# An attention and expert layer on one core: a rearranged prologue, with the layer norm applied by ScalarE

## The chip, the cores and the metric
The kernel runs on one core of a Trainium2 chip. The core has five engines, each with its own queue that runs in order: TensorE (PE, matmuls and transposes, with its weight loads PEld), VectorE (DVE), ScalarE (ACT), GpSimd (POOL) and SyncE (SP, which issues most DMAs). They wait for each other by semaphores. The metric is the device time of one execution in microseconds; the median of three runs of the kernel before is 842.51 us (841.69 to 844.74).

## The reference, cut to what matters
```python
mod = silu(c) @ wmod                       # c: (4, 256); six vectors of 256 per batch
sa, ca, ga, sb, cb, gb = ...               # ga, gb: sign kept, magnitude at least 0.25
h = layernorm(x) * (1 + ca) + sa           # x: (4, 512, 256)
q, k, v = (einsum('ihd,bpd->biph', W, h) for W in (W_Q, W_K, W_V))   # 16 heads of 128
attn = softmax(causal(k . q) / sqrt(128))  # 512 x 512 for each batch and head
x = x + ga * (W_O . (attn @ v))
h = layernorm(x) * (1 + cb) + sb
d = h @ down_w + down_b                    # to 128 columns
probs = softmax(h @ router_w + router_b - cost);  top 2 of 8 experts, gate = softmax(top)
# each of the 8 experts, hidden 128 to 512:
acc_e = gelu(gelu(d or 0) @ w1 + b1) @ w2 + b2
out = sum(gate * acc_e) + 0.1 * shared(d)
x = x + gb * (out @ up_w + up_b + gelu(h) @ core_w + core_b)
```
An expert that a token didn't choose still gives gelu(b1) @ w2 + b2 there; the kernel computes gelu(b1) once ("b1"), builds masked copies of it ("d0") and multiplies them with w2 ("dta", "dt").

## The kernel before, in words
All matmuls are fp32 products made of three fp32r matmuls (`mm3`, lines 679 to 682): each operand is held as a high part, written by ScalarE as a cast to fp32r, and a residual, written by VectorE or GpSimd as the difference. So nearly every product is followed by a ScalarE copy and a VectorE subtraction (L639 and L1049 for q, k, v and z; L619, L620 and L1035 for h; L609 with L532 or L987 for weights).

The work is a list of events (`plan`) made by `attention_plan` and `ffn_plan`. Every engine walks the same list and issues its own part of each event, so the list sets each engine's order. PSUM banks for events of `MISC` rotate over three: a product waits until the bank's use three before has been read.

The attention has 64 units (4 groups of 4 heads x 4 batches x 4 heads). A unit has: "q", "k" (PE), "v" (one half for each unit of a pair), "S" (scores in four row blocks; VectorE adds the mask and takes the row minimum at L1060, ScalarE exponentiates at L591), "ri" (reciprocal of the sums), "norm" (ScalarE scales the probabilities, L626), "ty" (VectorE transposes 32x32 blocks, L1076 to L1079), "tr" (four DMAs that complete the transpose, L462), "pt" (high part by ScalarE, L650; residual by GpSimd, L547), "z" (probabilities times v, PE) and "wo" (output product; VectorE multiplies by the gate ga, L1089, GpSimd adds to x, L540). Step i of the main loop has S(i+2), q(i+3), k(i+3), wo, v, pt(i+1), z(i) and tr(i+2); `pre` events stand ahead of z(i), `fill` groups after S, q, wo, z or v, and `post` events at the end.

A batch's layer norm is "st" 0 to 3 (VectorE's statistics L1004, L1009, L1013; GpSimd's power -1/2 at L490), "nm" 0 and 1 (VectorE writes (x - mean) * rstd to `tmp`, four instructions of 256 columns at L1025) and "h" 0 and 1 (PE transposes, L730; ScalarE applies scale and shift). "n" 0 to 3 are the batches' first norms, 4 to 7 their second. Norm 4 stands in step 55, norm 5 in step 59, norm 6 in step 62, just ahead of "dn 0" (the first batch's down projection, whose two gelus ScalarE does at L656 and L658 after loading another activation table). Norm 7 is in the expert stage.

The prologue's list is: b1, mod0, the statistics of batch 0, silu, wh0, wh1, nm, mod, h, wh2, then units 0 and 1 and wh3. "mod" makes the first layer's scale and shift, "ms" the second's and "mg" the gates ga and gb. For "mg" VectorE copies the product to `rows` (L974 to L977), and GpSimd then makes max(|g|, 0.25) with its sign in five dependent instructions (L497 to L505), writes it to DRAM with two DMAs, waits for them and issues the broadcast load (L508 to L511). "mg" and "ms" read the second part of wmod, which lies in x's place of batches 2 and 3; SP loads these batches after "ms". "mg" and batch 1's "h" come at the end of step 0, "ms" at the end of step 1. "wh n" and "ld n" take piece n of the weights through `stage`.

Before the first real product PE runs `warm(56)`, after "mod" `warm(4)` and after h(0) `warm(18)`: small bf16 matmuls on zeros.

Of the kernel before, what the change touches and what calls it, by code (L numbers as in the profile page):

```python
# [8 lines left out]
ALU = mybir.AluOpType  # L9
ACT = mybir.ActivationFunctionType  # L10
AX = mybir.AxisListType

B, S, D, H, DH = 4, 512, 256, 16, 128
# [4 lines left out]
EXPERT = [e for e, h in enumerate(HID) for _ in range(h // 128)]  # L18
LAG = 3
EULER = 2.718281828459045  # L20
WARM = 56, 4, 18
INV = 1.0 / float(DH) ** 0.5
BIG = 3.0e38

# [20 lines left out]
def attention_plan():  # L45

    pre, post = {}, {}
    fill = {}

    def put(where, i, *events):  # L50
        where.setdefault(i, []).extend(events)

    put(post, 0, ("mg",))
    put(post, 1, ("ms",))
    for b in (1, 2, 3):
        i = (0, 2, 5)[b - 1]
        if b == 1:
            fill[i] = [[("st", b, 0), ("st", b, 1)], [("st", b, 2)], [("st", b, 3)], [("nm", b, 0), ("nm", b, 1)]]
            put(post, i, ("h", b, 0), ("h", b, 1))
            continue  # L60
        fill[i] = [[("st", b, 0)], [("st", b, 1)], [("st", b, 2)], [("st", b, 3)]]
        fill[i + 1] = [[("nm", b, 0)], [("nm", b, 1)]]
        put(post, i + 1, ("h", b, 0))
        put(post, i + 2, ("h", b, 1))
    for n in range(4, 16):
        put(pre, 16 * (n // 4 - 1) + 5 + 2 * (n % 4), ("wh", n))
    for n in range(16, 20):
        put(pre, 34 + n, ("wh", n))
    fill[20] = [[("d0", 0)], [("d0", 1)], [], [], [("d0", 2)]]
    for b in range(2):  # L70
        fill[54 + 4 * b] = [[("st", B + b, k)] for k in range(4)]
        fill[55 + 4 * b] = [[("nm", B + b, 0)], [("nm", B + b, 1)]]
        put(post, 55 + 4 * b, ("h2", b, 0))
        put(post, 56 + 4 * b, ("h2", b, 1))
        put(post, 57 + 4 * b, ("r", b))
    fill[58] = [[("rs", 0, 1), ("rs", 0, 2)]] + fill[58]
    put(post, 58, *[("rp", 0, c) for c in range(4)])
    fill[59] += [[], [("rs", 0, 3)], [("rs", 0, 4)]]
    fill[60] = [[("rs", 0, k)] for k in range(5, 10)]
    fill[61] = [[("rs", 0, k)] for k in range(10, 15)]  # L80
    put(post, 61, ("wt", 0))
    fill[62] = [[("st", 6, 0), ("st", 6, 1)], [("st", 6, 2)], [("st", 6, 3)], [("nm", 6, 0), ("nm", 6, 1)]]
    put(post, 61, ("wh", 20), ("ld", 22))
    plan = [("b1",), ("mod0",)] + [("st", 0, k) for k in range(4)] + [("silu",), ("wh", 0), ("ld", 2), ("wh", 1), ("ld", 3),
            ("nm", 0, 0), ("nm", 0, 1), ("mod",),
            ("h", 0, 0), ("h", 0, 1), ("wh", 2), ("ld", 4), ("q", 0), ("k", 0), ("v", 0, 0), ("S", 0), ("ri", 0), ("norm", 0), ("ty", 0), ("q", 1), ("k", 1), ("v", 0, 1),
            ("S", 1), ("q", 2), ("ri", 1), ("k", 2), ("norm", 1), ("ty", 1), ("tr", 0), ("tr", 1), ("pt", 0), ("wh", 3)]
    loads = {0: [5]}
    for i, events in pre.items():
        for ev in events:  # L90
            if ev[0] == "wh":
                loads.setdefault(i + 1, []).append(ev[1] + 2)
    for i in range(NU):
        steps = list(fill.get(i, []))

        def add(*events):
            for ev in events:
                plan.append(ev)
                if steps and ev[0] in ("S", "q", "wo", "z", "v"):
                    plan.extend(steps.pop(0))  # L100

        if i + 2 < NU:
            add(("S", i + 2))
        if i + 3 < NU:
            add(("q", i + 3))
        if i + 2 < NU:
            add(("ri", i + 2))
        if i + 3 < NU:
            add(("k", i + 3))
        if i + 2 < NU:  # L110
            add(("norm", i + 2))
        if i >= 2:
            add(("wo", i // 2 - 1, i % 2))
        if i + 2 < NU:
            add(("ty", i + 2), ("v", i // 2 + 1, i % 2))
        if i + 1 < NU:
            add(("pt", i + 1))
        add(*pre.get(i, []))
        add(("z", i))
        if i + 2 < NU:  # L120
            add(("tr", i + 2))
        plan += [("ld", n) for n in loads.get(i, [])]
        plan += [ev for group in steps for ev in group]
        plan += post.get(i, [])
        if i + 2 == NU:
            plan.append(("dn", 0))
    return plan


def ffn_plan():  # L130
# [4 lines left out]
    def put(t, j, *events):  # L135
        at.setdefault((t, j), []).extend(events)
# [2 lines left out]
    put(0, 0, ("rs", 1, 1))  # L139
    put(0, 1, ("rs", 1, 2), ("wo", last, 0))  # L140
    put(0, 2, ("wo", last, 1), ("wl", 0), ("wl", 1))
    put(0, 3, ("wh", 22))
    put(0, 4, ("h2", 2, 0))
    put(0, 5, ("h2", 2, 1), ("wl", 2), ("wl", 3))
    for k, j in enumerate((6, 7, 8, 9)):
# [35 lines left out]
    plan, later = [], []  # L181
# [30 lines left out]
def build(nc, x, ct, wmod, wat, wfa, wfb, cst, bcol, b2, ub, cb, out, scr, scw):  # L212
    plan = attention_plan() + ffn_plan()
    use, rd = {}, {}
# [18 lines left out]
    with ExitStack() as ctx:  # L233
# [3 lines left out]
        def sem(name):  # L237
            return ctx.enter_context(nc.semaphore(name))
# [3 lines left out]
        X = sb("X", 4096)  # L242
        tmp = sb("tmp", 1024)
        fb = sb("fb", 1024)
        stage = sb("stage", 2048)
        cc = sb("cc", C_END)
# [6 lines left out]
        mv = sb("mv", 8 + 24)  # L253
        rs = sb("rs", 16)
        sm = sb("sm", 4)
        nb = sb("nb", 4)
        ri = sb("ri", 4)
# [32 lines left out]
        mask = cc[:, C_MASK:C_MASK + 512]  # L290

        s_x = [sem(f"s_x{b}") for b in range(B)]
        s_ct, s_wm, s_wm2, s_c, s_b, s_bc, s_g, s_gb = (sem(n) for n in ("s_ct", "s_wm", "s_wm2", "s_c", "s_b", "s_bc", "s_g", "s_gb"))
        s_st = [sem("s_st0"), sem("s_st1")]
        s_wh, s_wl, s_wd = sem("s_wh"), sem("s_wl"), sem("s_wd")
        s_sil, s_mod, s_mc, s_gr, s_gd = (sem(n) for n in ("s_sil", "s_mod", "s_mc", "s_gr", "s_gd"))
        mf, mh, me = sem("mf"), sem("mh"), sem("me")
# [4 lines left out]
        s_ve, s_r0, s_xn = sem("s_ve"), sem("s_r0"), sem("s_xn")  # L302
# [25 lines left out]
        def wt(slot, at, n):  # L328
            return W[slot][:, at:at + n], W[slot][:, 4096 + at:4096 + at + n]
# [73 lines left out]
        def piece_after(n):  # L403
# [3 lines left out]
                return ("wo", 8 * (n // 4) - 9, 1)  # L407
            return ("v", NU // 2 - 1, 1)

        block = ctx.enter_context(nc.Block())  # L410


        @block.sync
        def _(sp):
# [4 lines left out]
            def load_x(b):  # L419
                sp.dma_start(X[:, b * 1024:b * 1024 + 1024], x[:, b * 1024:b * 1024 + 1024]).then_inc(s_x[b], 16)  # L420

            load_x(0)
            load(0)
            sp.dma_start(cc[:, 0:128], cst[:, 0:128]).then_inc(s_id, 16)
            load(1)
            sp.dma_start(cc[:, 128:], cst[:, 128:]).then_inc(s_c, 16)
            for ev in plan:
                if ev[0] == "ms":
                    sp.wait_ge(mf, use[ev] + 1)
# [2 lines left out]
                elif ev[0] == "wh":  # L432
                    n = ev[1]
                    if n == 2:
                        sp.dma_start(X[:, 2048:4096], wmod[:, 1024:3072]).then_inc(s_wm2, 16)
                        load_x(1)
                elif ev[0] == "ld":
                    n = ev[1]
                    sp.wait_ge(s_wl, n - 2) if n > 2 else sp.wait_ge(s_wd, 1)
# [138 lines left out]
        def _(act):  # L578
# [16 lines left out]
            for ev in plan:  # L595
# [7 lines left out]
                elif kind == "wh":  # L603
# [3 lines left out]
                    if piece_after(n):  # L607
                        act.wait_ge(mf, use[piece_after(n)] + 1)
                    act.copy(wt(slot, a, w)[0], stage[:, (n % 2) * 1024:(n % 2) * 1024 + w]).then_inc(s_wh, 1)  # L609
                elif kind in ("h", "h2"):  # L610
                    _, b, k = ev
                    o = 0 if kind == "h" else 16
# [268 lines left out]
        def _(v):  # L881
# [75 lines left out]
                v.tensor_tensor(sil[:, 16:24], sil[:, 16:24], sil[:, 0:8], ALU.mult).then_inc(s_sil, 1)  # L957


            tmp_read = [use[("h", b, 1)] + 1 for b in range(B)] + [use[("h2", b, 1)] + 1 for b in range(B)]  # L960
            xv = 0
            for ev in plan:
                kind = ev[0]
# [27 lines left out]
                elif kind == "st":  # L991
# [3 lines left out]
                    if k == 0:  # L995
                        if n < B:
                            v.wait_ge(s_x[b], 16)
                        else:
                            v.wait_ge(s_y, 2 * (25 + 2 * b) + 2)
                        if n:  # L1000
                            v.wait_ge(s_xn, 2 * n)
                    if k < 2:
                        for c in (2 * k, 2 * k + 1):
                            ins = v.bn_stats(mv[:, 8 + 6 * c:14 + 6 * c], X[:, b * 1024 + 256 * c:b * 1024 + 256 * c + 256])  # L1004
                        ins.then_inc(s_st_, 1)
                    elif k == 2:
                        v.wait_ge(s_st_, 3 * n + 2)
                        for c in range(4):
                            ins = v.bn_aggr(mv[:, 2 * c:2 * c + 2], mv[:, 8 + 6 * c:14 + 6 * c])  # L1009
                        ins.then_inc(s_st_, 1)  # L1010
                    else:
                        v.wait_ge(s_st_, 3 * n + 3)
                        v.tensor_scalar(rs[:, 0:4], mv[:, 1:8:2], 1e-5, None, ALU.add).then_inc(s_ve, 1)  # L1013
                elif kind == "nm":

                    _, n, k = ev
                    b = n % B
                    dst = stage[:, 0:1024] if n == 7 else tmp[:]
                    if n == 7:
                        v.wait_ge(s_wd, 3)  # L1020
                    elif n:
                        v.wait_ge(mf, tmp_read[n - 1])
                    v.wait_ge(s_r0, n + 1)
                    for c in (2 * k, 2 * k + 1):
                        ins = v.tensor_scalar(dst[:, 256 * c:256 * c + 256],  # L1025
# [255 lines left out]
```

## Time and profile before
| | us |
|---|---|
| median of 3 runs | 842.51 (841.69 to 844.74) |
| profiled execution, its own time | 843.71 |
| its span, first to last instruction | 841.9 |
| mean granted TensorE clock | 0.978 |

Durations below come from the profiled execution. A timeline row is: start, duration, engine, line, operation, output<-input, shapes, number of instructions merged, and in brackets how long the engine had been idle and what released it. Clock 1.00 is 2.4 GHz, 0.50 is 1.2 GHz.

### The profile page before, as it was taken

What the parts mean: (1) busy time and instruction counts of PE and PEld (TensorE: products, weight loads), DVE (VectorE), ACT (ScalarE), POOL (GpSimd) and SP (SyncE); (2) the same over time, 40 slices, a digit from 0 to 9 for tenths busy, and PEclk for the clock granted to TensorE, in tenths of its full rate; (3) what the DMA queues carried; (4) which work ended last, traced back from release to release, by engine and by line L of the source; (5) the groups of instructions that cost most, each with busy time, mean ns of one, the idle gap of its engine ahead of it and who ended that gap; (6) DMA issues with size and microseconds to landing.
All of it is one profiled execution on the core that took longest, in us unless ns stands there. A gap on an engine that the chain in (4) does not pass through costs nothing.

```text
span 841.9 us, 14484 instructions
## 1 busy us (share of the span) xinstructions
PE 800.9 (95%) x4822; PEld 713.0 (85%) x4822; DVE 680.8 (81%) x1639; ACT 628.3 (75%) x1404; POOL 450.2 (53%) x311
## 2 busy tenths in 40 slices
PE   7778999999999999999999999999999599999997
PEld 6657978999999999999999999998998587788786
DVE  4686998888888888888888788889898787877776
ACT  4566778878887788788887887787877488686874
POOL 3064455664444655544466544575465555566753
PEclk7979999999999999999999999999999799999999
DMA  7233223334222433332234332344222220212131
GB/s 243 72 89 107 63 63 88 88 97 111 63 64 65 112 94 88 91 89 66 64 89 108 100 88 63 78 107 129 65 63 64 69 84 18 76 51 80 47 114 38
DMA packets 47449, 70.54 MB, mean 84 GB/s; under 512 B 5520, under 2 KB 38448, under 8 KB 47248
## 3 DMA queue, kind: packets, MB, share of 16 engines
q1 hardware_dynamic: 46720, 68.28, 30.8%
q0 software_dynamic: 368, 0.81, 0.3%
q8 instruction: 39, 0.64, 0.3%
q10 hardware_dynamic: 288, 0.53, 0.2%
q14 instruction: 34, 0.28, 0.1%
HBM read 25.49 MB, written 2.17 MB: 33 GB/s over the span
## 4 chain that ended last, share of the span: by engine, by line
PE 75%; ACT 9%; DVE 8%; issue 3%; POOL 2%; DMA 2%; SPq 0%; DVEq 0%; POOLq 0%; ACTq 0%
PE M L681 16%; PE M L680 16%; PE M L682 16%; PE S L680 7%; PE S L682 6%; PE S L681 6%; ACT PB L591 3%; PE T L680 2%; PE T L682 2%; PE T L681 2%; ACT PB L626 1%; DVE tmp L1025 1%; DVE S L1060 1%; DVE gab L1076 1%; ACT pth L650 1%
## 5 line engine op out<-in xcount | busy, mean ns | idle before, releaser
L547 POOL TENSOR_TENSOR ptl<-ptl,pth 128x640 fp32r<-128x640 f32 x128 | 198.9, 1576 | 45.0 <-ACT pth L650 45.0
L591 ACT ACTIVATE PB<-S,nb 128x128 f32<-128x128 f32 (+3 forms) x256 | 133.8, 532 | 114.0 <-DVE nb L1060 114.0
L540 POOL TENSOR_TENSOR X<-X,fb 128x512 f32<-128x512 f32 x64 | 83.2, 1301 | 252.1 <-DVE fb L1089 252.1
L626 ACT ACTIVATE PB<-PB,ri 128x256 f32<-128x256 f32 (+3 forms) x256 | 124.4, 579 | 9.4 <-DVE ri L1069 9.3
L1049 DVE TENSOR_TENSOR qk<-M,qk 128x512 fp32r<-128x512 f32 x128 | 88.1, 689 | 53.5 <-ACT qk L639 53.5
L1060 DVE CUSTOM_DVE_ANT_0 S<-S,cc 128x128 f32<-128x128 f32 (+3 forms) x256 | 117.5, 521 | 2.3 <-PE S L682 2.3
L1076 DVE STREAM_TRANSPOSE gab<-PB 128x256 f32<-128x256 f32 (+2 forms) x192 | 109.5, 623 | 1.1 <-ACT PB L626 0.6
L680 PE MATMUL M<-hh,W 128*128 128x512 f32 x264 | 103.8, 393 | 0.2 <-DVE hl L1035 0.2
L681 PE MATMUL M<-hl,W 128*128 128x512 f32 x264 | 103.3, 391 | 0.0
L682 PE MATMUL M<-hh,W 128*128 128x512 f32 x264 | 103.1, 391 | 0.0
L680 PE MATMUL S<-qk 128*128 128x128 f32 (+3 forms) x256 | 88.0, 344 | 4.6 <-DVE qk L1049 4.6
L650 ACT CAST pth<-ptl 128x640 fp32r<-128x640 f32 x128 | 87.7, 743 | 3.5 <-DMA ptl<-gab 3.5
L673 ACT ACTIVATE Gr<-S,bc 128x512 fp32r<-128x512 f32 x84 | 58.5, 696 | 34.3 <-PE S L682 34.3
L682 PE MATMUL S<-qk 128*128 128x128 f32 (+3 forms) x256 | 83.5, 326 | 0.0
L681 PE MATMUL S<-qk 128*128 128x128 f32 (+3 forms) x256 | 83.4, 326 | 0.0
L681 PE MATMUL M<-ptl,vh 128*128 128x512 f32 (+3 forms) x256 | 83.4, 326 | 0.0
L682 PE MATMUL M<-pth,vl 128*128 128x512 f32 (+3 forms) x256 | 83.0, 324 | 0.0
L1203 DVE TENSOR_TENSOR Gr<-S,Gr 128x512 fp32r<-128x512 f32 x84 | 57.4, 687 | 31.2 <-ACT S L674 29.1
L680 PE MATMUL M<-pth,vh 128*128 128x512 f32 (+3 forms) x256 | 81.0, 316 | 1.6 <-DVE qk L1049 1.1
L639 ACT CAST qk<-M 128x512 fp32r<-128x512 f32 x128 | 75.9, 594 | 6.7 <-PE M L682 6.4
L680 PE MATMUL M<-W,hh 128*128 128x256 f32 x256 | 73.6, 287 | 6.5 <-DVE qk L1049 6.1
L681 PE MATMUL M<-W,hh 128*128 128x256 f32 x256 | 72.7, 284 | 0.0
(181 smaller groups left out, 2310.5 us busy)
## 6 DMA issues: line engine op xcount, KB each, us to landing
ptl<-gab SPq DMA_DIRECT2D x256, 160.0 KB, 3.1
stage<-in_wat SPq DMA_DIRECT2D x16, 512.0 KB, 4.9
gab<-scw SPq DMA_DIRECT2D x16, 256.0 KB, 3.3
tmp<-scw SPq DMA_DIRECT2D x16, 256.0 KB, 3.5
X<-in_x SPq DMA_DIRECT2D x4, 512.0 KB, 5.3
stage<-in_wfa SPq DMA_DIRECT2D x3, 512.0 KB, 4.4
out<-X SPq DMA_DIRECT2D x3, 512.0 KB, 2.6
X<-in_wmod SPq DMA_DIRECT2D x1, 1024.0 KB, 6.5
```

The lines of the kernel that those rows point to most:

```text
L540: pool.tensor_tensor(X[:, a:a + 512], X[:, a:a + 512], fb[:, c2 * 512:c2 * 512 + 512], ALU.add).then_inc(s_y, 1)
L547: pool.tensor_tensor(ptl[u % 2][:, s], ptl[u % 2][:, s].bitcast(F32), pth[u % 2][:, s].bitcast(F32), ALU.subtract).then_inc(s_pl, 1)
L591: ins = act.activation(PB[:, P_OFF[i]:P_OFF[i] + w], PS[bk][:, a:a + w], ACT.Exp, bias=nb[:, i:i + 1], scale=-1.0, accum_out=sm[:, i:i + 1])
L626: act.activation(p, p, ACT.Copy, scale=ri[:, i:i + 1]).then_inc(s_P3, 1)
L639: act.copy(dst, src).then_inc(mh, 1)
L650: act.copy(pth[u % 2][:, s], ptl[u % 2][:, s].bitcast(F32)).then_inc(s_ph, 1)
L680: pe.matmul(o, lhs[0], rhs[0], start=start, stop=False, **kw)
L681: pe.matmul(o, lhs[0], rhs[1], start=False, stop=False, **kw)
L682: return pe.matmul(o, lhs[1], rhs[0], start=False, stop=stop, **kw)
L1049: v.tensor_tensor(lo, src, hi.bitcast(F32), ALU.subtract).then_inc(me, 1)
L1060: ins = v.tensor_tensor_reduce(PS[bk][:, a:a + w], PS[bk][:, a:a + w], mask[:, 512 - w:512], -INV, BIG, ALU.add, ALU.min, nb[:, i:i + 1])
L1076: v.transpose(Y_blocks(i, i + 1), P_blocks(i, 0, i + 1))
```

## The change
- "b1" leaves the head of the list and is done in the expert stage, at chunk 3; the three "d0" operations move from step 20 to chunks 5 to 7.
- x of batch 0 is loaded in two halves with a semaphore each; the identity is loaded ahead of the first weight piece; x of batch 1 is loaded with the first transfers.
- The layer norm is applied by ScalarE for norms 0 to 6: a new event "nb" has VectorE compute -mean * rstd for the four row blocks, and "nm" is then four ScalarE activations with scale and bias from `rs`. Norm 7 stays on VectorE.
- Batch 1's statistics and norm go into the prologue; its h half 0 stands ahead of z(0), half 1 at the end of step 0, after "ms".
- "mg" goes into the prologue, behind v(0,1) and ahead of wh3 and pt(0); "ms" goes to the end of step 0.
- In the prologue v(0,0) and v(0,1) come after "ty", tr(0) right after v(0,0), and wh1 stands behind the norm of batch 0.
- The warm-up counts are 60, 4, 12.

```diff
-WARM = 56, 4, 18
+WARM = 60, 4, 12
...
-    put(post, 0, ("mg",))
-    put(post, 1, ("ms",))
+    put(post, 0, ("ms",))
     for b in (1, 2, 3):
         i = (0, 2, 5)[b - 1]
         if b == 1:
-            fill[i] = [[("st", b, 0), ("st", b, 1)], [("st", b, 2)], [("st", b, 3)], [("nm", b, 0), ("nm", b, 1)]]
-            put(post, i, ("h", b, 0), ("h", b, 1))
+            put(pre, i, ("h", b, 0))
+            put(post, i, ("h", b, 1))
             continue
         fill[i] = [[("st", b, 0)], [("st", b, 1)], [("st", b, 2)], [("st", b, 3)]]
-        fill[i + 1] = [[("nm", b, 0)], [("nm", b, 1)]]
+        fill[i + 1] = [[("nb", b), ("nm", b, 0)], [("nm", b, 1)]]
...
-    fill[20] = [[("d0", 0)], [("d0", 1)], [], [], [("d0", 2)]]
...
-        fill[55 + 4 * b] = [[("nm", B + b, 0)], [("nm", B + b, 1)]]
+        fill[55 + 4 * b] = [[("nb", B + b), ("nm", B + b, 0)], [("nm", B + b, 1)]]
...
-    fill[62] = [[("st", 6, 0), ("st", 6, 1)], [("st", 6, 2)], [("st", 6, 3)], [("nm", 6, 0), ("nm", 6, 1)]]
+    fill[62] = [[("st", 6, 0), ("st", 6, 1)], [("st", 6, 2)], [("st", 6, 3)], [("nb", 6), ("nm", 6, 0), ("nm", 6, 1)]]
...
-    plan = [("b1",), ("mod0",)] + [("st", 0, k) for k in range(4)] + [("silu",), ("wh", 0), ("ld", 2), ("wh", 1), ("ld", 3),
-            ("nm", 0, 0), ("nm", 0, 1), ("mod",),
-            ("h", 0, 0), ("h", 0, 1), ("wh", 2), ("ld", 4), ("q", 0), ("k", 0), ("v", 0, 0), ("S", 0), ("ri", 0), ("norm", 0), ("ty", 0), ("q", 1), ("k", 1), ("v", 0, 1),
-            ("S", 1), ("q", 2), ("ri", 1), ("k", 2), ("norm", 1), ("ty", 1), ("tr", 0), ("tr", 1), ("pt", 0), ("wh", 3)]
+    plan = [("mod0",)] + [("st", 0, k) for k in range(4)] + [
+        ("silu",), ("nb", 0), ("wh", 0), ("ld", 2), ("nm", 0, 0), ("nm", 0, 1), ("wh", 1), ("ld", 3), ("mod",),
+        ("h", 0, 0), ("h", 0, 1), ("st", 1, 0), ("st", 1, 1), ("wh", 2), ("ld", 4),
+        ("q", 0), ("st", 1, 2), ("st", 1, 3), ("k", 0), ("nb", 1), ("nm", 1, 0), ("nm", 1, 1), ("S", 0),
+        ("q", 1), ("ri", 0), ("k", 1), ("norm", 0), ("ty", 0), ("v", 0, 0), ("tr", 0),
+        ("S", 1), ("q", 2), ("ri", 1), ("k", 2), ("norm", 1), ("ty", 1), ("v", 0, 1), ("mg",),
+        ("wh", 3), ("tr", 1), ("pt", 0)]
...
-    put(0, 3, ("wh", 22))
+    put(0, 3, ("wh", 22), ("b1",))
+    for k in range(3):
+        put(0, 5 + k, ("d0", k))
...
-            load_x(0)
+            for n, done in enumerate((s_x[0], s_xh)):
+                sp.dma_start(X[:, 512 * n:512 * n + 512], x[:, 512 * n:512 * n + 512]).then_inc(done, 16)
+            sp.dma_start(cc[:, 0:128], cst[:, 0:128]).then_inc(s_id, 16)
             load(0)
-            sp.dma_start(cc[:, 0:128], cst[:, 0:128]).then_inc(s_id, 16)
             load(1)
             sp.dma_start(cc[:, 128:], cst[:, 128:]).then_inc(s_c, 16)
+            load_x(1)
...
                     if n == 2:
                         sp.dma_start(X[:, 2048:4096], wmod[:, 1024:3072]).then_inc(s_wm2, 16)
-                        load_x(1)
...
+                elif kind == "nm" and ev[1] < 7:
+                    _, n, k = ev
+                    b = n % B
+                    act.wait_ge(s_nb, n + 1)
+                    if n and k == 0:
+                        act.wait_ge(mf, tmp_read[n - 1])
+                    for c in (2 * k, 2 * k + 1):
+                        s = slice(b * 1024 + 256 * c, b * 1024 + 256 * c + 256)
+                        ins = act.activation(tmp[:, 256 * c:256 * c + 256], X[:, s], ACT.Identity,
+                                             bias=rs[:, 8 + c:9 + c], scale=rs[:, 4 + c:5 + c])
+                    ins.then_inc(s_xn, 1)
...
+                    if n == 0 and k == 1:
+                        v.wait_ge(s_xh, 16)
...
+                elif kind == "nb":
+                    n = ev[1]
+                    v.wait_ge(s_r0, n + 1)
+                    v.scalar_tensor_tensor(out=rs[:, 8:12], in0=mv[:, 0:8:2], scalar=-1.0, in1=rs[:, 4:8],
+                                           op0=ALU.mult, op1=ALU.mult).then_inc(s_nb, 1)
```

## Rows read from the trace of the kernel before

**Rows 1.** the page's busy time, share of the span, instructions of each engine
```profile
PE 800.9 (95%) x4822; PEld 713.0 (85%) x4822; DVE 680.8 (81%) x1639; ACT 628.3 (75%) x1404; POOL 450.2 (53%) x311
```

**Rows 2.** busy us (x instructions) of PE, PEld, DVE, ACT, POOL; clock, DMA, GB/s
```profile
34.00:36.00 2.00, 2.00 (x7) 1.81 (x8) 0.58 (x3) 0.00 (x0) 0.00 (x0) 0.50 0.90 223
...
100.00:200.00 100.00, 97.22 (x613) 88.15 (x613) 86.30 (x207) 79.94 (x192) 54.66 (x35) 1.00 0.35 87
...
680.00:690.00 10.00, 9.27 (x46) 7.27 (x45) 8.70 (x16) 9.99 (x18) 3.82 (x4) 1.00 0.43 131
```

**Rows 3.** timeline (start, us, engine, line, output<-input, idle before), prologue
```profile
11.10 1.04 ACT L609 CAST W<-stage 128x1024 fp32r<-128x1024 f32 x1 [0.72 <-DMA stage<-in_wat]
11.56 3.49 DVE L1025 TENSOR_SCALAR tmp<-X,mv,rs 128x256 f32<-128x256 f32 x4
...
19.12 0.69 DVE L1035 TENSOR_TENSOR hl<-M,hh 128x512 fp32r<-128x512 f32 x1 [0.65 <-ACT M L620]
```

**Rows 4.** the DMA issued within 1.1 to 1.3 us; last: us to landing
```profile
stage<-in_wat SPq DMA_DIRECT2D x1, 512.0 KB, 7.2
```

**Rows 5.** timeline of PE, 26 to 100 us
```profile
33.30 0.48 PE L680 MATMUL S<-qk 128*128 128x128 f32 x1 [2.96 <-DVE qk L1049]
...
47.70 0.50 PE L680 MATMUL M<-pth,vh 128*128 128x512 f32 x1
...
57.50 1.94 PE L730 MATMUL M<-cc,tmp 128*128 128x128 f32 x8 [5.85 <-DVE tmp L1025]
...
69.35 1.90 PE L719 MATMUL M<-sil,X 128*128 128x4 f32 x16
...
80.32 0.38 PE L680 MATMUL M<-W,hh 128*128 128x256 f32 x1 [2.92 <-DVE qk L1049]
```

**Rows 6.** timeline of POOL (GpSimd), 10 to 100 us
```profile
43.10 3.11 POOL L547 TENSOR_TENSOR ptl<-ptl,pth 128x640 fp32r<-128x640 f32 x2 [20.66 <-ACT pth L650]
46.17 2.40 POOL L532 TENSOR_TENSOR W<-stage,W 128x1024 fp32r<-128x1024 f32 x1
...
58.53 1.95 POOL L497 TENSOR_SCALAR gab<-rows 4x512 f32<-4x512 f32 x1 [1.97 <-DVE rows L977]
...
69.17 0.57 POOL L511 DMA_DIRECT2D gab<-scr  x1 [1.37 <-DMA scr<-rows]
```

**Rows 7.** timeline of DVE (VectorE), 27 to 650 us
```profile
43.95 0.26 DVE L1060 CUSTOM_DVE_ANT_0 S<-S,cc 128x128 f32<-128x128 f32 x1
...
57.68 0.67 DVE L977 COPY rows<-M 4x512 f32<-4x512 f32 x1
...
62.10 0.29 DVE L1060 CUSTOM_DVE_ANT_0 S<-S,cc 128x128 f32<-128x128 f32 x1
...
78.92 0.75 DVE L1004 BATCH_NORM_STATS2 mv<-X 128x6 f32<-128x256 f32 x2 [4.65 <-DMA X<-in_x]
...
86.67 0.29 DVE L1060 CUSTOM_DVE_ANT_0 S<-S,cc 128x128 f32<-128x128 f32 x1
...
121.98 2.19 DVE L1025 TENSOR_SCALAR tmp<-X,mv,rs 128x256 f32<-128x256 f32 x2
...
648.58 0.28 DVE L1060 CUSTOM_DVE_ANT_0 S<-S,cc 128x128 f32<-128x128 f32 x1
```

**Rows 8.** ACT (ScalarE) groups by form: busy us, mean ns, idle before
```profile
L626 ACT ACTIVATE PB<-PB,ri 128x256 f32<-128x256 f32 x64 | 34.5, 539 | 9.4 <-DVE ri L1069 9.3
...
L619 ACT ACTIVATE hh<-M,modt 128x512 fp32r<-128x512 f32 x16 | 12.7, 794 | 11.5 <-PE M L730 10.6 <-POOL X L540 0.9
```

**Rows 9.** timeline of ACT, POOL, DVE and PE at the hand-over
```profile
667.46 1.28 ACT L656 ACT_TABLE_LOAD   x1
...
670.04 1.02 POOL L490 TENSOR_TENSOR rs<-rs 128x4 f32<-128x4 f32 x1
...
671.17 1.38 DVE L1025 TENSOR_SCALAR tmp<-X,mv,rs 128x256 f32<-128x256 f32 x4 [2.52 <-POOL rs L490]
...
673.21 0.50 PE L680 MATMUL S<-ur,W 128*128 128x512 f32 x1 [0.86 <-DVE ur L1189]
```

More of the change, by code:

```diff
@@ L292, in build @@
         s_x = [sem(f"s_x{b}") for b in range(B)]
+        s_xh, s_nb = sem("s_xh"), sem("s_nb")
         s_ct, s_wm, s_wm2, s_c, s_b, s_bc, s_g, s_gb = (sem(n) for n in ("s_ct", "s_wm", "s_wm2", "s_c", "s_b", "s_bc", "s_g", "s_gb"))
@@ L408, in piece_after @@
             return ("v", NU // 2 - 1, 1)
+        tmp_read = [use[("h", b, 1)] + 1 for b in range(B)] + [use[("h2", b, 1)] + 1 for b in range(B)]
         block = ctx.enter_context(nc.Block())
@@ L957, in silu @@
                 v.tensor_tensor(sil[:, 16:24], sil[:, 16:24], sil[:, 0:8], ALU.mult).then_inc(s_sil, 1)
-            tmp_read = [use[("h", b, 1)] + 1 for b in range(B)] + [use[("h2", b, 1)] + 1 for b in range(B)]
             xv = 0
@@ L1013, in _ @@
                         v.tensor_scalar(rs[:, 0:4], mv[:, 1:8:2], 1e-5, None, ALU.add).then_inc(s_ve, 1)
-                elif kind == "nm":
+                elif kind == "nb":
[3 more added lines that the diff above has]
+                                           op0=ALU.mult, op1=ALU.mult).then_inc(s_nb, 1)
+                elif kind == "nm" and ev[1] == 7:
                     _, n, k = ev
                     b = n % B
[L1018 to L1022, printed above, removed]
+                    dst = stage[:, 0:1024]
+                    v.wait_ge(s_wd, 3)
                     v.wait_ge(s_r0, n + 1)
```

## The prediction
> **What bounds the kernel now.** I read the busy shares first. The tensor engine is busy for 95% of the span [rows 1], so what can be won is PE's idle time and the time it runs at half clock. Then the table of stretches: from 100 to 200 us PE is busy for 97.22 of 100 us, at full clock, while ScalarE (ACT) has 79.94 and VectorE (DVE) 86.30 [rows 2]. So between about 90 and 650 us the order of PE's own work sets the pace, and a change on another engine counts there only where it starves PE. Third, the chain of waits and PE's own timeline for the first 100 us, where PE stands still four times for reasons that this change touches:
> - before its first real matmul: the first batch's transposed layer norm is ready only when the last VectorE residual starts at 19.12 us, that is at 19.8 [rows 3];
> - 2.96 us before unit 1's scores, behind a k residual [rows 5];
> - 5.85 us before the transposes of batch 1, behind its layer norm [rows 5];
> - 2.92 us before a v product; its cause is VectorE's 4.65 us wait for batch 2 of x to land, with the k residual queued behind it [rows 5, 7].
> After the stop of 2.96 us PE's granted clock is 0.50, 1.2 GHz in place of 2.4 (34 to 36 us) [rows 2].
> Last, the hand-over from attention to experts, from 666 us. PE's first expert matmul starts at 673.21 us and waited for VectorE's residual of the down projection [rows 9].
>
> **The change, part by part.** The profiled execution took 843.71 us (span 841.9 us and 1.8 around it), 1.2 above the median of the three runs. I work out a difference, and add it to the median.
>
> *Start.* The gelu of b1 and its activation table leave the head of ScalarE's queue; the exp of silu now comes first. The copy of weight piece 0 can start when its piece has landed, at 1.2 + 7.2 = 8.4 us [rows 4]. Two issues and the identity now stand ahead of this load, so I take 8.7. Copy (1.04, as piece 1's) to 9.7, then ScalarE applies the layer norm. The trace has no ScalarE instruction of that form. Bounds: 539 ns for 256 columns with a scale alone, 794 ns for 512 columns with bias and scale [rows 8]; four lie between 2.0 and 3.2 us, and as neighbours overlap by some 0.1 us I take 2.0, nearest to the 256-column row. VectorE's four took 3.49 us here [rows 3]. The norm ends at 11.7 in place of 15.05. ScalarE then does the copy of piece 1 (it landed at 11.1, copy 1.04 [rows 3]) to 12.7, and the two halves of h follow as before. The last residual ends at 16.4 in place of 19.8: 3.4 us gained.
> The Trainium skill, "ScalarE: Activation LUTs", section "What ACT_TABLE_LOAD costs", gives 186 ns + 0.833 ns per element and about 93 ns per pointer operand. By that one of these would be an estimated 585 ns, four 2.1 us with its overlap of 93 ns; the 794 ns of the 512-column row agree (its formula gives 799).
>
> *Up to unit 1.* Batch 1's statistics (two pairs, 1.4 us) and its norm lie beside PE's q, k and scores. Because "v" goes behind the scores and transposes, unit 1's scores no longer stand behind a k residual that waited for the transposes: the 2.96 us go. VectorE's transposes of unit 1 ended at 43.95, where unit 2's scores start [rows 7]; now 43.95 - 3.4 - 2.9 = 37.7.
>
> *The gate.* "mg" now comes right there: v residual 0.65, two small operations and the copy of the gate rows (0.67 [rows 7]), 1.1 in all: ends at 39.4. From this copy's end (57.68 + 0.67 = 58.35) to the last of GpSimd's gate instructions (69.17 + 0.57 = 69.74 [rows 6]) go 11.4 us: five operations, two transfers out, a wait for them, one transfer back. GpSimd's queue is in order. Before, that stretch lay between the probability residuals of unit 1 and those of unit 2 and held up little. Now piece 3's residual (2.40) and unit 0's probability residuals (3.11) are queued behind it [rows 6]: 39.4 + 11.4 + 2.4 + 3.1 = 56.3. PE's first attention product z(0), which ran at 47.70 [rows 5], waits for them. So it starts 8.6 us later than before, after some 13 us of idle PE and at half clock. This is a new wait, worth more than each of those removed.
>
> *From z(0) to unit 3's scores on VectorE.* Before: 47.70 to 62.10, 14.4 us, with the 5.85 us wait for batch 1's norm in it [rows 5, 7]; that wait goes, as the norm was made in the prologue. After: z(0) has 3 x 1280 columns, at 1.2 GHz 3.3 us; the second modulation product 2.6 (1.90 at full clock [rows 5], twice that at half; I take a clock that rises in between); four transposes 0.7, a third of the eight at 57.50 (1.94); then ScalarE and VectorE on h half 1, 2.1: 8.7 us, to 65.0. Against 62.10 that is 2.9 us late; all that the start gained is spent.
>
> *Units 3 and 4.* The modulation is read out of x's place a unit earlier, so batch 2's load is issued at about 63 and lands by 69, before VectorE asks (about 76). From unit 3's to unit 5's scores it was 86.67 - 62.10 = 24.6 us. A unit without a stop: (648.58 - 86.67)/58 = 9.69 us [rows 7]. Two are 19.4: 5.2 gained. Net at unit 5: -2.3 us.
>
> *Norms of batches 2, 3 and of the second layer norm.* ScalarE 2.0 us more in four units (with h its queue holds 11.7 us in such a unit against 9.69), VectorE 1.4 less (1.38 for four at 671.17 [rows 9]) up to 4.4 less (2.19 for two beside GpSimd [rows 7]). PE buffers a unit. I take +0.3; bounds -2 and +4 (one us each way per unit, the full difference of 11.7 and 9.7 being 2).
>
> *Hand-over.* Batch 2's second norm. GpSimd's pow runs 670.04 to 671.06, then VectorE normalised 671.17 to 672.47, and ScalarE meanwhile loaded gelu's table at 667.46 and did the down projection's gelus [rows 9]. Now the norm stands in ScalarE's queue ahead of that: it waits for the small VectorE operation to 671.3, takes 2.0 to 673.3, table 1.28, two gelus 1.3, residual 0.6: PE's first expert matmul starts at 676.5 in place of 673.21, 3.3 late. PE then has idled 4.3 us, more than the 2.96 after which it was seen at half clock; at half clock its next two to three products cost 1.2 more. From 680 to 690 ScalarE is busy for 9.99 of 10 us and PE for 9.27 [rows 2], so little is caught up: 0.5. +4.0 us; bounds +1 and +6. If the shift reached no end it would be 0.
>
> *Gelu of b1 and the three "d0" operations* among the experts: 0.2 on ScalarE, under 1 on VectorE, both with slack; +0.2. The warm-up matmuls (60 and 12 for 56 and 18) move within idle time, 0; bounds -0.7 and +1 (a head of PE at half clock).
>
> Sum: -2.3 + 0.3 + 4.0 + 0.2 = +2.2, the profiled execution to 845.9, the median to 844.7. 0.5% is 4.2 us, about what a measurement of this kernel tells from no change: my forecast is no measurable change.
>
> **Rivals.**
> A. *The gate hides on GpSimd* (its operations run quicker beside an idle VectorE, or the copy comes earlier). Then z(0) starts at 43 to 50, and each us is a us of time: from -3 to -13 at unit 3. For it: GpSimd has been idle for 20.66 us when unit 0's probabilities reach it at 43.10 [rows 6]. Against: 3.4 of the 11.4 us are transfers, and the copy needs unit 1's transposes. With a third of it hidden, -8: 836.5. Chance 0.15.
> B. *The hand-over's delay is absorbed*: PE was idle 0.86 there and stops again later, ScalarE has room after 690. +1 in place of +4: 841.5. Chance 0.2.
> C, on the other side: *ScalarE becomes the bound in each unit that holds a norm.* Place: behind unit scores 5, 8, 57, 61; the norm delays the exponentials, these the k copy and the normalised probabilities. It decides as soon as PE's lead is used up: then each costs 11.7 - 9.7 = 2.0 less what VectorE's relief gives, some +1.3, 5 in all: 849.5. For it: the queue's 11.7 against 9.69. Against: ScalarE is busy for 80% only from 100 to 200 us [rows 2], and a lead of PE carries a late unit over. Chance 0.2. The Trainium skill, "ScalarE: Activation LUTs", "Rules for kernel authors", says adds and multiplications belong on VectorE; by that rule this rival holds. The trace agrees only where GpSimd rests: 1.38 us for four on VectorE at 671.17 [rows 9], 3.49 beside GpSimd's and others' work [rows 3].
> Forecast: 0.45.
>
> **Numbers.** Faster by over 0.5% (below 838.3): A's 0.13 and 0.05 of B and the forecast, 0.18. Slower by over 0.5% (above 846.7): C 0.17 and 0.07 of the forecast, 0.24. Within: 0.58. The range reaches to A and C and holds the bounds of the norm and the hand-over: 835.5 to 850.0; the forecast's own is 841 to 848.
>
> **What would show it.** VectorE's first h residuals end near 16.4; the gate copy at 39; GpSimd's gate run ends near 51; PE idle some 12 us up to z(0) near 56, at 0.50 clock after it; no stop of VectorE for x; unit 5's scores near 84.4; four ScalarE norms of 0.5 us each near 671, and the table load behind them; first expert matmul 1.3 us later in the span than before (674.5). Wrong, if z(0) starts before 52, if the first expert matmul's distance to the end of attention doesn't grow, or if PE idles in units 3 and 6.

## The result and the profile after

The changed kernel takes 858.9 us (median of 4 runs, 855.3 to 859.6), the kernel before 842.9 us: ratio 1.0176, 95% interval 1.0154 to 1.0197. It is 16 us slower by the medians. I had forecast 844.7 us, no measurable change, in a range from 835.5 to 850.0; the time is 8.9 us above its upper end.

The profiled execution took 859.18 us against 843.71, so the two traces, 15.5 us apart, show nearly the whole of it. First the page of the profile: PE's busy share, and its granted clock in 40 slices of 21.4 us.

```profile
span 857.4 us, 14481 instructions
PE 807.3 (94%) x4820; PEld 717.1 (84%) x4820; DVE 664.5 (77%) x1618; ACT 640.4 (75%) x1431; POOL 449.5 (52%) x311
PEclk8958999999999999999999999999998788999999
```

Before, the line of the clock was:

```profile
PEclk7979999999999999999999999999999799999999
```

PE is busy 6.4 us longer than before [rows 1] for the same products: part of the loss is work at half clock, in slices 3 and 4 (43 to 86 us) and 31 to 34 (643 to 729 us). PE's longest waits in the new kernel (total, times, longest):

```profile
PE M L699 <- POOL ptl L554: 13.6, 2, 13.1
PE M L878 <- DVE wg L969: 9.2, 2, 7.1
PE M L699 <- DVE qk L1072: 7.4, 9, 0.9
PE S L699 <- DVE ur L1212: 4.4, 1, 4.4
```

The first and the fourth are new at this length (before, the same two were 0.5 and 0.9 us). The waits of 2.96, 5.85 and 2.92 us of before [rows 5] are gone, as is VectorE's of 4.65 us for x [rows 7].

To see where time is lost I follow one set of events through every trace: the start of PE's first attention product z(0), of VectorE's first score operation of units 3, 5 and 63, and of ScalarE's first gelu of expert chunks 0, 9 and 15. It is read from timelines; the last column is the end of the span.

```
                     z(0)   unit 3  unit 5  unit 63  chunk 0  chunk 9  chunk 15   span
before               47.70   62.10   86.67   648.58   674.21   689.38    703.10  841.9
changed              57.09   67.27   86.94   650.95   680.76   697.33    718.55  857.4
later by              9.39    5.17    0.27     2.37     6.55     7.95     15.45   15.5
```

So the attention up to its last unit costs 2.4 us, the hand-over to the experts 5.6 more (4.2 to chunk 0, 1.4 to chunk 9), and 7.5 come in a stretch where I had expected 0.2. GpSimd's timeline in the first 100 us shows the gate ahead of the probabilities:

```profile
40.44 1.95 POOL L504 TENSOR_SCALAR gab<-rows 4x512 f32<-4x512 f32 x1 [18.56 <-DVE rows L995]
...
51.03 0.57 POOL L518 DMA_DIRECT2D gab<-scr  x1 [1.36 <-DMA scr<-rows]
51.62 2.35 POOL L539 TENSOR_TENSOR W<-stage,W 128x1024 fp32r<-128x1024 f32 x1
53.92 6.01 POOL L554 TENSOR_TENSOR ptl<-ptl,pth 128x640 fp32r<-128x640 f32 x4
```

These answer to [rows 6]. PE's timeline, against [rows 5, 9]:

```profile
57.09 0.77 PE L699 MATMUL M<-pth,vh 128*128 128x512 f32 x1 [13.08 <-POOL ptl L554]
...
679.07 0.79 PE L699 MATMUL S<-ur,W 128*128 128x512 f32 x1 [4.42 <-DVE ur L1212]
...
699.03 0.25 PE L865 MATMUL M<-g0z,W 128*128 128x16 f32 x1 [1.31 <-issue]
```

The hand-over on VectorE (-mean * rstd) and ScalarE, against [rows 9]:

```profile
673.40 0.16 DVE L1038 SCALAR_TENSOR_TENSOR rs<-mv,rs 128x4 f32<-128x4 f32 x1 [2.43 <-POOL rs L497]
673.60 2.07 ACT L626 ACTIVATE tmp<-X,rs 128x256 f32<-128x256 f32 x4 [3.84 <-DVE rs L1038]
675.69 1.28 ACT L675 ACT_TABLE_LOAD   x1
680.76 0.69 ACT L692 ACTIVATE Gr<-S,bc 128x512 fp32r<-128x512 f32 x1 [2.02 <-PE S L701]
```

And the stretches of the new loss (columns as in [rows 2]; the eighth number, ahead of the DMA share, is the clock), with the VectorE instruction that PE waited for at 699.03, the last of "d0" (the trace names no releaser there; in the kernel `dta` waits for that instruction's semaphore, and it ends at 698.93):

```profile
50.00:60.00 10.00, 2.91 (x9) 2.66 (x10) 0.00 (x0) 0.00 (x0) 8.88 (x6) 0.50 0.16 53
60.00:70.00 10.00, 10.00 (x42) 9.44 (x42) 3.43 (x12) 3.02 (x7) 0.00 (x0) 0.52 0.70 195
690.00:700.00 10.00, 8.45 (x42) 6.31 (x41) 9.23 (x17) 8.67 (x15) 3.81 (x3) 1.00 0.41 134
700.00:710.00 10.00, 10.00 (x41) 8.89 (x41) 3.09 (x10) 2.48 (x4) 7.48 (x6) 0.55 0.08 28
710.00:720.00 10.00, 9.99 (x37) 6.85 (x37) 4.74 (x11) 4.95 (x8) 1.29 (x1) 0.77 0.02 9
730.00:740.00 10.00, 7.83 (x33) 5.46 (x33) 9.64 (x20) 7.72 (x14) 6.63 (x5) 1.00 0.12 39
```

```profile
697.92 1.01 DVE L1134 TENSOR_TENSOR g0z<-g,g0z 128x160 fp32r<-128x160 f32 x1
```

From 700 to 710 PE is busy all the time, ScalarE and VectorE are idle two thirds of it and more, and the clock is 0.55: PE does its products at half clock.

### The profile page after: what moved, and what is told of

Its sections match the earlier page's. It is cut to its first block, busy times and chain, and to the rows that moved or that the text cites. A ratio compares the mean times of both kernels' runs of the same rounds, so it can differ in the third digit from the quotient of the medians.

```text
span 857.4 us, 14481 instructions
## 1 busy us (share of the span) xinstructions
PE 807.3 (94%) x4820; PEld 717.1 (84%) x4820; DVE 664.5 (77%) x1618; ACT 640.4 (75%) x1431; POOL 449.5 (52%) x311
## 4 chain that ended last, share of the span: by engine, by line
PE 72%; ACT 13%; DVE 9%; issue 3%; POOL 2%; DMA 1%; SPq 0%; DVEq 0%; ACTq 0%; POOLq 0%
PE M L699 15%; PE M L700 15%; PE M L701 15%; PE S L699 6%; PE S L701 6%; PE S L700 6%; ACT PB L598 4%; PE T L699 2%; PE T L701 2%; PE T L700 2%; ACT qk L658 2%; DVE S L1083 2%; ACT tmp L626 2%; DVE gab L1099 1%; ACT PB L645 1%
## 5 line engine op out<-in xcount | busy, mean ns | idle before, releaser
L699 PE MATMUL M<-pth,vh 128*128 128x512 f32 (+3 forms) x256 | 81.4, 318 | 17.2 <-POOL ptl L554 13.6
L699 PE MATMUL M<-W,hh 128*128 128x256 f32 x256 | 73.1, 286 | 3.9 <-DVE qk L1072 3.9
L699 PE MATMUL M<-W,zt 128*128 128x256 f32 x256 | 72.9, 285 | 0.0
```

The costliest lines, as they stand in the source:

```text
L699: pe.matmul(o, lhs[0], rhs[0], start=start, stop=False, **kw)
```

## The experiments

Times are medians; each was measured beside the kernel before, whose medians were 843.0 to 844.1. The differences are to the changed kernel's 858.9. The event times in the tables are those of one profiled execution of each kernel, and these differ by chance too: in kernels whose prologue is the same, unit 0's scores start on VectorE between 21.4 and 23.0 us, latest in the changed kernel's profile. So what one edit does is read from the stretch in which it acts, beside the median.

**Undoing one part each, and all three.**

```diff
# x1: b1 at the head, d0 in step 20
+    plan = [("b1",), ("mod0",)] + [
...
+    fill[20] = [[("d0", 0)], [("d0", 1)], [], [], [("d0", 2)]]
-    put(0, 3, ("wh", 22), ("b1",))
-        put(0, 5 + k, ("d0", k))
# x2: norm 6 on VectorE
-                elif kind == "nm" and ev[1] < 7:
+                elif kind == "nm" and ev[1] not in (6, 7):
...  (VectorE does these, and the "nb" of norm 6 goes)
# x3: the gate at the end of step 0
-    put(post, 0, ("ms",))
+    put(post, 0, ("mg",), ("ms",))
...
-        ... ("ty", 1), ("v", 0, 1), ("mg",),
+        ... ("ty", 1), ("v", 0, 1),
```

> The changed kernel with b1 at the head of the list and the three d0 operations in step 20 again; all else as changed. Theory 1 (the clock): in the changed kernel the second d0 residual ends at 698.9 us, PE waits 1.31 us for it ahead of the masked products, and its clock falls for the 14 us after; with the operands ready long before, that wait and the half clock go and the stretch from expert chunk 9 to 15 shrinks by 6 to 7.5 us, against 1 or 2 us more at the head for the table load: 852 to 854. Rival (the hand-over): the clock falls because of PE's 4.42 us stop at 674 to 679 and what follows; then the stretch at 701 to 715 stays at half clock and the time stays at 858 to 861.

> The changed kernel with norm 6 alone on VectorE again, as before the change. Theory: ScalarE's queue at the hand-over (norm 2.07 us, then the table load) costs 4.2 us up to the first expert gelu and 1.5 more at half clock behind it; both go: the first gelu comes 2.3 us later than in the kernel before in place of 6.5, and the time falls by 4 to 6: 853 to 855 with the fall of the clock at the masked products still there. Rival: the fall of the clock at 701 us is a late effect of the hand-over's stop; then it goes too and the time is 845 to 848.

> The changed kernel with the gate event moved from the prologue to the end of step 0, ahead of ms. Theory: GpSimd's 11.4 us for the gates stand ahead of unit 0's probabilities and cost PE the 13.1 us wait before z(0); with them behind, z(0) starts at 44 to 46, unit 3's scores on VectorE at 52 to 57 in place of 67.3, and the time falls by 8 to 12: 847 to 851. Rival: the wait only moves, because the gate's run now stands ahead of unit 1's or 2's probabilities; then unit 5's scores come no more than 4 us earlier: 855 or more.

> The three undone together (b1 and d0 early, norm 6 on VectorE, gate at the end of step 0). If the three are separate costs, the sum of the three single differences within 3 us: about 836 to 841, faster than the kernel before (842.9) by 2 to 7. If two of them share one cause (the clock), it is less than the sum by 5 or more: 843 or above.

```
                     z(0)   unit 3  unit 5  unit 63  chunk 0  chunk 9  chunk 15   median
x1 d0 back           56.26   66.45   86.18   650.61   680.29   696.68    710.14   852.0
x2 norm 6 on VectorE 55.90   66.09   85.22   649.40   674.37   689.53    704.42   848.5
x3 gate back         43.36   52.78   72.43   636.48   666.61   683.47    701.61   844.1
x4 all three         42.10   51.75   70.62   636.92   662.80   677.96    691.69   832.5
```

x1 is 6.9 us faster, as theory 1 had it, and its rival falls: the hand-over's stop stays (4.42 us), yet chunk 9 to 15 takes 13.5 us, not 21.2, and the clock stays up there. (Its profiled run has 3 us at half clock later, from 724 us, worth 1.5 us; so the median gains less than the stretch.) From x1, the same stretches:

```profile
690.00:700.00 10.00, 9.89 (x53) 8.30 (x54) 8.46 (x20) 8.65 (x16) 4.61 (x4) 1.00 0.38 114
700.00:710.00 10.00, 10.00 (x58) 7.79 (x56) 4.44 (x10) 5.58 (x10) 6.61 (x5) 1.00 0.09 29
```

x2 is 10.4 us faster, more than my 4 to 6. Unit 63 to chunk 9 is 40.1 us in place of 46.4, and in the profiled run, the fastest of four (846.6 to 850.1), the fall of the clock is avoided as well (chunk 9 to 15: 14.9 us), though a stop for d0 is still there. PE's timeline of x2:

```profile
673.37 0.50 PE L700 MATMUL S<-ur,W 128*128 128x512 f32 x1 [0.86 <-DVE ur L1216]
...
691.15 0.25 PE L866 MATMUL M<-g0z,W 128*128 128x16 f32 x1 [0.96 <-issue]
```

So the rival was half right: the fall goes with the hand-over's stop, though x1 shows that this stop alone doesn't bring it. (The stop for d0 is also shorter here, 0.96 us in place of 1.31; the two aren't separated.) The two losses overlap. The three single gains sum to 32.1 us, all three together give 26.5. The overlap lies in the stretch from chunk 9 to 15: there x1 saves 7.8 us, x2 6.3 and x3 3.1, 17.2 in all, and the three together 7.5. So the fall of the clock is counted more than once. The excess of 5.6 us is beyond the 3 us I allowed for separate costs, as my second expectation had it; but 832.5 us is below the times that I gave for either, as I had both x2 and x3 too small.

x3 is 14.8 us faster, more than expected, and its rival falls. Unit 5 comes 14.5 us earlier, and the gain is kept to the end. The stop for d0 is still 1.30 us here, but the half clock behind it lasted 7 us in place of 14. GpSimd's timeline of x3, and PE's z(0):

```profile
37.78 2.40 POOL L539 TENSOR_TENSOR W<-stage,W 128x1024 fp32r<-128x1024 f32 x1 [16.72 <-ACT W L616]
40.14 3.07 POOL L554 TENSOR_TENSOR ptl<-ptl,pth 128x640 fp32r<-128x640 f32 x2
45.34 3.04 POOL L554 TENSOR_TENSOR ptl<-ptl,pth 128x640 fp32r<-128x640 f32 x2 [2.13 <-ACT pth L669]
49.76 1.95 POOL L504 TENSOR_SCALAR gab<-rows 4x512 f32<-4x512 f32 x1 [1.39 <-DVE rows L995]
```

```profile
43.36 0.47 PE L699 MATMUL M<-pth,vh 128*128 128x512 f32 x1 [1.18 <-POOL ptl L554]
```

The gate's run now falls where GpSimd has nothing that PE waits for.

**Which part of the gate.** The same, but only GpSimd's instructions move; PE's product and VectorE's copy stay in the prologue.

```diff
-    put(post, 0, ("ms",))
+    put(post, 0, ("mp",), ("ms",))
-                if ev[0] == "mg":
+                if ev[0] == "mp":
```

> The changed kernel with only GpSimd's part of the gate (five operations and three transfers) moved behind unit 1's probabilities, at the end of step 0; PE's product and VectorE's copy stay in the prologue. Theory (GpSimd's queue alone makes the 13.1 us wait): as with the whole gate event moved: z(0) at 43 to 45, unit 5's scores at 72 to 74, 843 to 846. Rival (PE's and VectorE's parts, or the place of the copy behind unit 1's transposes, take part in it): z(0) after 47 or 848 and more.

845.0 us, z(0) at 45.83, unit 5 at 72.91. It is GpSimd's queue; the place of the other parts is worth under 1 us in the median, though z(0) starts 2.5 us later than in x3, 0.8 past what I expected. The rival falls. The hand-over's stop (4.44 us) and the stop for d0 are as in the changed kernel, but in this profiled run the half clock behind them lasted only 3 us, and chunk 9 to 15 took 16.5 us. PE's timeline of x11:

```profile
684.67 0.25 PE L866 MATMUL M<-g0z,W 128*128 128x16 f32 x1 [1.31 <-issue]
```

**What lets the clock fall at 701 us.**

```diff
# x7 (14) and x10 (30): PE busy while it waits for d0
+                        pe.wait_ge(me, use[("dt",)] - 2)
+                        for _ in range(14):
+                            pe.matmul(o[:, 256:384], Dz[:], Dz[:], start=True, stop=True)
                         pe.wait_ge(s_gz, 1)
-                        pe.wait_ge(me, use[("dt",)] - 2)
# x8: the masked products one chunk later
-        put(0, 9 + c, ("dta", c))
+        put(0, 10 + c, ("dta", c))
-    put(0, 12, ("dt",), ("nm", 7, 0))
+    put(0, 13, ("dt",), ("nm", 7, 0))
```

> The changed kernel with 14 dummy matmuls (128x128 bf16 on zeros, into a free part of the same bank) in the place where PE waits 1.31 us for d0 ahead of the first masked products. The wait stays as long, but PE is busy in it; the later work is the same. Theory (the stop lets the clock fall): from the gelu of chunk 9 to that of chunk 15 it is 14 to 15.5 us in place of 21.2 and the time falls by 5 to 7. Rival (the 40 narrow products, 16 columns each, let it fall by themselves): it stays at 20 us or more and the time within 2 us of the changed kernel's.

> The changed kernel with the masked products (dta, dt) one chunk later, so that d0 is ready. Theory: no stop, no fall of the clock: chunk 9 to 15 in 13.5 to 14.5 us, 7 off the time, as with d0 back in step 20 but without the early table load: 851 to 853. Rival: with less than 1.31 us gained the stop shrinks, but the fall comes all the same, since PE has stops and narrow products close by: 856 or more.

> As the changed kernel with dummy matmuls in the stop ahead of the masked products, but 30 of them, to cover the whole 1.31 us (14 left 0.48 us of it, and the runs fell between 849.5 and 858.6). Theory (the stop lets the clock fall): with none left all runs lie at 850 to 854 and from chunk 9's gelu to chunk 15's it is 14 to 15.5 us. Rival (where the stop lies in time, or the narrow products by themselves, decide, and PE's record before them): runs spread over 849 to 859 again.

x7: 853.8 us, but its four runs spread over 849.5, 852.6, 854.9 and 858.6, and in the profiled one chunk 9 to 15 took 16.5 us. The gain of 5.1 us is what the theory gave, the stretch is longer than it gave; the rival's numbers don't hold. The dummies had left part of the stop, and about 3 us at half clock followed it:

```profile
696.39 0.95 PE L862 MATMUL M<-Dz 128*128 128x128 bf16 x14
697.82 0.28 PE L867 MATMUL M<-g0z,W 128*128 128x16 f32 x1 [0.48 <-DVE g0z L1136]
```

x10 fills it. PE's timeline and its stretch in x10:

```profile
694.99 1.85 PE L862 MATMUL M<-Dz 128*128 128x128 bf16 x30
696.65 0.26 PE L867 MATMUL M<-g0z,W 128*128 128x16 f32 x1
```

```profile
700.00:710.00 10.00, 9.99 (x56) 7.70 (x56) 4.53 (x11) 5.44 (x10) 5.85 (x5) 1.00 0.07 27
```

850.7 us, all six runs between 849.6 and 852.5; chunk 9 to 15 in 15.2 us. Not a microsecond of waiting was removed, only PE's idleness in it. The median is 8.3 us lower, but not all of that is the edit's: in the profiled run 6.0 us are gained from chunk 9 to 15, and 2.6 lie ahead of chunk 9, where the two kernels are the same. x8, where d0 is ready in time and nothing is filled, gives 851.8 us (850.2 to 853.1) and 14.1 us for the stretch, 7.2 less, with the same narrow products. So the products of 16 columns don't let the clock fall by themselves.

**The late d0 alone, in the kernel before.**

```diff
-    plan = [("b1",), ("mod0",)] + ...
+    plan = [("mod0",)] + ...
-    put(0, 3, ("wh", 22))
+    put(0, 3, ("wh", 22), ("b1",))
+    for k in range(3):
+        put(0, 5 + k, ("d0", k))
```

> The kernel before with only the gelu of b1 and the three d0 operations moved to the expert stage, as in the change (the table load leaves the head). Theory: the stop ahead of the masked products comes here too, about 1 us, and the head gains 1 to 2: if the clock holds, as it did with norm 6 undone, 841 to 844; if it falls, 847 to 850. What decides is where the fall needs ScalarE's delay ahead of it. Rival: there is no stop at all without the change's other parts, 840 to 842.

Nine runs have a median of 843.1 us, ratio 1.0007 (0.9979 to 1.0036): no difference. A tenth took 1556.9 us; what held it I can't say (with it the median is 844.2). The profiled execution, the fastest of all (839.8 us), had a stop of 0.96 us and kept its clock behind it. The head gained more than my 1 to 2 us. ScalarE no longer waits for the biases and a first table load ahead of silu, and the norm on VectorE came before GpSimd's first weight piece, so that its four instructions took 1.38 us in place of 3.49 [rows 3] (in the kernel before, one of the four took 2.52 us, while GpSimd worked for 2.35):

```profile
10.25 1.38 DVE L1026 TENSOR_SCALAR tmp<-X,mv,rs 128x256 f32<-128x256 f32 x4
```

The last h residual ended at 16.59 us in place of 19.81, and unit 5 came at 80.60 in place of 86.67; of these 6.1 us, 3.9 were left at the end. The runs spread from 839.8 to 849.3, three of them at 848 to 849 with a mean clock of 0.970 to 0.972 in place of 0.976 to 0.982. By these the clock falls for longer in some runs here too, but only one was profiled, so the place in the others isn't shown. The rival (no stop at all) falls.

**The stops and the half clock side by side.** The two stops of PE in each profiled run, how long the granted clock was 0.50 behind the second (read in windows of 1 us), and the stretch from chunk 9 to 15:

```
                 hand-over   stop for d0             half clock   chunk 9 to 15
changed            4.42      1.31                      14 us          21.2
x3                 4.57      1.30                       7             18.1
x11                4.44      1.31                       3             16.5
x7                 4.34      0.48 behind 14 dummies     3             16.5
x10                4.42      filled by 30 dummies       0             15.2
x1                 4.42      none                       0             13.5
x8                 4.42      none                       0             14.1
x2                 0.86      0.96                       0             14.9
x6                 0.69      0.96                       0             14.9
before             0.86      none                       0             13.7
```

In these profiles the clock falls only where both stops are there, and then for very different times behind the same stop. The loss of 7.5 us in the changed kernel's profile is the largest of the four. Each row is one execution, and in x2 and x6 the second stop is also the shorter one, so that both are needed isn't shown.

**Norms on VectorE, and the fastest version.** x9 is x4 with norms 2 to 5 on VectorE as well; x12 is x9 with b1 and d0 in the expert stage and the masked products one chunk later.

```diff
-                elif kind == "nm" and ev[1] < 7:
+                elif kind == "nm" and ev[1] not in (2, 3, 4, 5, 6, 7):
...  (VectorE does these; "nb" goes for norms 2 to 6)
```

> The version with the three undone (832.5 us) and norms 2 to 5 on VectorE too; ScalarE keeps norms 0 and 1 in the prologue. Theory: on ScalarE each of the norms 4 and 5 costs 1.0 us more than on VectorE and 2 and 3 little: from unit 5's scores to unit 63's 562 us in place of 566.3 in that version, the time 829 to 831. Rival: norms on VectorE meet GpSimd's work and starve PE as in the kernel before: no difference (831 to 834).

> The fastest version (gate at the end of step 0, norms 2 to 6 on VectorE, 829.2 us), but with b1 and d0 in the expert stage as in the change and the masked products one chunk later, so that PE doesn't wait for d0. Theory: with the operands in time their place costs nothing, and the gelu table load is gone from the head, worth at most the 1.3 us it takes: 827.5 to 830, no difference that three rounds can show. Rival (the late d0 costs by VectorE's load or the clock still falls in some runs): 832 or more.

```
                     z(0)   unit 3  unit 5  unit 6  unit 57  unit 58  unit 63  chunk 0   median
before               47.70   62.10   86.67   98.01   584.09   595.47   648.58   674.21   842.9
changed              57.09   67.27   86.94   99.35   584.41   596.80   650.95   680.76   858.9
x4                   42.10   51.75   70.62   84.58   570.35   582.77   636.92   662.80   832.5
x9                   43.76   53.43   72.79   85.02   570.99   582.38   635.50   660.39   829.2
```

x9 takes 829.2 us, ratio to the kernel before 0.9818 (0.9786 to 0.9849): 14.7 us faster than it, and 3.2 faster than x4, as expected, though the two intervals of the ratio to the kernel before touch (x4: 0.9841 to 0.9894). From unit 5's scores to unit 63's it is 562.7 us against 566.3. Of this 1.7 lie in unit 5, where x4's profile is also longer at half clock (7 us against 3), so that part isn't the norm's alone; units 57 and 61 give 1.0 and 1.1. Unit 57 to 58, which holds norm 4, takes 12.4 us with the norm on ScalarE (x4, changed) and 11.4 on VectorE (x9, before). x12 takes 829.7 us, ratio 0.9818 (0.9797 to 0.984): with its operand in time, the late d0 costs nothing.

## Why the prediction was wrong, step by step

- *Start:* right in its parts, 1.2 us too early. ScalarE took 2.07 us for the four parts of a norm (forecast 2.0). The last h residual ends at 16.93 + 0.69 = 17.6 (forecast 16.4): piece 0 landed only at 9.8, 1.1 later than I took. So 2.2 us were gained, not 3.4. Little of this needed the norm on ScalarE: x6, with only b1 gone from the head, had the residual done at 16.6. From the start of piece 0's copy to that residual's end it was 10.5 us before, 8.6 in x6 and 7.8 in the changed kernel. The Trainium skill, "ScalarE: Activation LUTs", section "What ACT_TABLE_LOAD costs", gave an estimated 2.1 us for the four; the trace agrees.
- *The gate:* right in mechanism and nearly in size: forecast z(0) at 56.3 after some 13 us idle, measured 57.09 after 13.08. Undone in two ways (x3, x11), it is shown.
- *z(0) to unit 3:* 8.7 forecast, 10.2 measured. I let the clock rise in the middle; it stayed at 0.50 to some 69 us. Unit 3 was 5.2 late, not 2.9.
- *Units 3 to 5:* 5.2 gained forecast, 4.9 measured. Net at unit 5: +0.3 against my -2.3.
- *Norms in the attention:* "+0.3" measured +2.1 to unit 63. My rival C had the mechanism: three of the four units with a norm took 1.0 to 1.1 us longer (5, 57, 61; 12.2 to 12.4 us), and unit 8, where VectorE had worked beside GpSimd [rows 7], 0.5 less. In unit 57 ScalarE was busy for 10.5 us in place of 8.6, and PE stood still for 1.8 us in place of 0.9. My 11.7 us for its queue was 1.2 too much, and the cost was about 1 us in each of the three, not C's 1.3 in all four. The Trainium skill's advice to put adds and multiplications on VectorE ("ScalarE: Activation LUTs", "Rules for kernel authors") holds in these three and in x9; in the prologue x6 agrees, with 1.38 us on VectorE, ahead of GpSimd's work, against 2.07 on ScalarE.
- *Hand-over:* 4.0 forecast, 5.6 measured. PE's first expert matmul came 3.5 us late (forecast 3.3), after a stop of 4.42 (forecast 4.3). At half clock the first gelu lost 0.7 more and the chunks up to 9 another 1.4 (forecast 1.2 in all), and the 0.5 that I let be caught up wasn't. Rival B (absorbed) is refuted; x2 shows the cause.
- *Gelu of b1 and d0:* this is the step that failed: "0.2 on ScalarE, under 1 on VectorE, both with slack; +0.2". In the profiled run it measured 7.5 us. I priced the moved operations by their engines' slack, and didn't ask who waits for their result and when. VectorE is in order and full there (9.23 of 10 us busy): the third d0 operation ended at 698.9, PE had reached the masked products 1.3 us before. Even that wait is worth only 1.3 us; the rest is PE's clock, down to 1.2 GHz for the 14 us after. x1, x8 and x10 each take a different part of that chain away, and the stretch gives back 7.8, 7.2 and 6.0 us (the medians fall by 6.9, 7.2 and 8.3).

Errors of +2.6, +1.8, +1.6 and +7.3 us make up the 13.3 between my +2.2 and the trace's +15.5. With the last one right I would have forecast 852.0, still 6.9 too low: all four errors had one sign. In two of them, at z(0) and at the hand-over, I had taken the half clock for shorter than it was. Small slips in the working don't bear on this: A's and B's times are 0.2 us too low for their differences to 844.7, and four of eight transposes were taken as a third of their time, not half.

What stays open: what decides how long the half clock lasts behind the same stop of 1.31 us (14, 7 or 3 us), whether a stop of 0.96 us would bring it behind the hand-over's 4.4 us one, and whether that one is needed. The length of a stop alone doesn't decide. A stop of 2.16 to 2.18 us ahead of a small transpose, behind chunk 15, stands in all thirteen profiled runs. In the changed kernel it is at 732.3 and passes with the clock at 1.00 (730 to 740), as in the kernel before and five others; in x1, x2, x6, x7, x8 and x11 some 3 us at half clock follow it, which makes x1's and x2's rest of the span 1.5 us longer.

## What to carry to other kernels

When an operation moves to a later place, look for the first reader of its result on every engine and compare the two times; slack on its own engine says nothing of that. Ahead of an in-order queue, a long chain with transfers in it (here 11.4 us of gates on GpSimd) delays all that stands behind, so it belongs where the next entry isn't awaited; moved alone, it gave back 14.8 us of a change that had looked worthless. A short stop of a busy TensorE can cost several times its length through the clock (here up to 7.5 us for 1.3), and by very different amounts from run to run, so one profile shows only one case of it: x7's runs, with 0.48 us of the stop left, spread over 9 us. Filling the stop with dummy products shows the clock's part without moving anything else.

## What I had not expected of the hardware

- A stop of 1.31 us, with narrow products behind it, was followed by half clock from about 701 to 714.7 us (0.55, then 0.77 by stretches), while PE was busy without a break. In two variants the same stop was followed by 7 and by 3 us of it.
- After the 13 us stop the clock was still 0.52 over 60 to 70 us, with PE busy for all of it: it came back some 12 us after the work did.
- Thirty dummy matmuls (1.85 us) that fill a wait of the same length took 6.0 us off the stretch behind it.
- Four instructions of the norm took 1.38 us on VectorE with GpSimd idle, and 3.49 where GpSimd began a piece among them.
